# The one-hot rows of the edges' lanes: made by ScalarE in nine operations, or by VectorE in one

## The chip, the cores and the metric

One core of a Trainium2 chip runs the whole program. The metric is the device time of one execution in microseconds (us). Besides TensorE (matmul), VectorE, ScalarE and GpSimd work beside each other, and DMA queues bring data in and out. In profiles they stand as PE (PEld for its weight loads), DVE, ACT, POOL and SP.

## What is computed

The reference is one layer of a graph transformer on 6250 nodes with 512 features and 100,000 edges. Cut to what matters here:

```python
xn = layernorm(x)
h = relu(xn @ W1 + b1) @ W2 + b2
gnn = h + segment_sum(h[dst], src, 6250)          # a sum over each node's edges
x = x + gnn + attention_and_mlp(xn)               # Performer attention, then an MLP with gelu
x = x + haar_ffn(layernorm(x))                    # the tail
```

The edge sum is done on relu(xn @ W1 + b1), which has 256 columns, and W2 is applied afterwards. The rows of the table are gathered for 128 edges at a time, and a matmul with a one-hot matrix adds them to their nodes: row e of that matrix has a 1 in the column of edge e's node within its tile of 125 nodes (its lane), and 0 elsewhere.

## The kernel before

The nodes are handled in 25 steps of 250. **Phase 1** (until about 470 us) makes the k side of the attention and the table of hidden rows, while VectorE sorts the edges by their node. A short **turn** follows. **Phase 2** (531 to 1118 us) makes q, v and y, **phase 3** (1141 to 1751 us) the MLP, and a **tail** the Haar part.

The sorted edges form 440 groups of two times 128 edges (PAIRS); four groups are a batch (BP = 4), and there are 110 batches. A group goes like this. GpSimd gathers its rows into a ring of 12 slots (L592). TensorE multiplies them by two one-hot matrices of 128x125 in float16 (`groups`, L833 to L836), into one of two banks by turns. VectorE adds the bank to the accumulator at an offset read from memory (`add_groups`, L1655). TensorE may start group n when the add of group n-2 is done.

The one-hot matrices of a batch are eight, and stand in one of two buffers `hit`. VectorE makes them all in one compare, 128x1000 (`one_hots`, L1637): the lane numbers 0 to 124 (`iota_h`) against the edges' lanes (`lane_of`). It makes batch q+2 right after the add of the last group of batch q. An edge that has no place in the tile has a lane outside of 0 to 124, and so a row of zeros.

From the turn on each step has eight groups, spread over it. In a step u of phase 2 TensorE's order is: V products (L858 to L860; the first waits for the first y rows of the step before), groups 0 and 1 between and behind them, the first half of the next q products (L721 to L723 and L708 to L710), groups 2 and 3, transposes of q' (L876), the second half of the q products with groups 4 and 5, the y products (L888), and groups 6 and 7 among them. VectorE's order is: the chain that scales q', the adds of groups 0 to 4, `low_parts` (L1432), which splits off the low half of x for step u+2, the reads of the q products (L1556, L1548), the add of group 5, the first y rows (L1756), the add of group 6, the second y rows, the add of group 7, and the row statistics (L1680). With eight groups a step, one compare stands behind the add of group 3 and one behind that of group 7.

ScalarE's order in a step is: two exps (L1147), the copy of the transposed q', called qpT, out of its bank (L1239), and the cast of x's high half for step u+2 (`high_parts`, L1157). `low_parts` waits for that cast. All engines work through their instructions in the order in which they are written.

In phase 3 ScalarE makes norm rows (L1226), two pairs of gelus (L1250) and the copies of the transposed rows (L1139). TensorE makes features (L940) and mlp2 (L949), with groups between. From step 23 on the tail's work joins: copies (L1257, L1262, L1266), gelus (L1272, `tail_gelus`), and the scaling of rows (L1280, `scaled_rows`). There the first mlp2 products of a step also wait for the tail's gelus.

Of the kernel before, what the change touches and what calls it, by code (L numbers as in the profile page):

```python
# [88 lines left out]
TURN, SECOND, BETWEEN, THIRD, LAG = pair_counts()  # L89
LAST = STEPS + LAG  # L90
# [26 lines left out]
def build_program(nc, d):  # L117
    ctx = ExitStack()
    with ctx:
# [111 lines left out]
        row_of, lane_of = in_edge(PAIRS, 2, dt=I32), in_edge(PAIRS, 2, dt=F16)  # L231
# [12 lines left out]
        eps_c = const(2)  # L244
# [72 lines left out]
        def rows(t):  # L317
# [29 lines left out]
        (h_rows, tr, h_t, feat, feat_c, r_up, r_ok, kadd, hk_mm, qn, qt, qtc,  # L347
         y_mm, y_read, zadd, z_ok, m_mm, hits, g_mm, g_add, x_high) = (sem(n) for n in (
            "h_rows", "h_transposed", "hT", "features", "features_copied", "r_read", "r_rows", "kp_added",
# [276 lines left out]
        def _(pe):  # L626
# [195 lines left out]
            def groups(count):  # L822

                for n in range(group_at[0], group_at[0] + count):
                    if n % BP == 0:
                        pe.wait_ge(hits, n // BP + 2)
                    pe.wait_ge(gathered[n % RING], 32 * (n // RING + 1))
                    if n >= 2:
                        pe.wait_ge(g_add, n)
                    for h in (0, 1):  # L830
                        bk, one_hot, row = (BE, BH)[n % 2], hit[n // BP % 2][:, n % BP * 2 + h, :], ring_h[:, n % RING * 2 + h]
                        if h == 0:
                            pe.matmul(bk[0:P, 0:RW], one_hot, row[:, LOW_AND_ONE], start=True, stop=False)  # L833
# [281 lines left out]
        def _(act):  # L1115
# [75 lines left out]
            for t in each_step(1):  # L1191
# [10 lines left out]
                act.activation(acc[0:P, t.u * 2:t.u * 2 + 2, 0:HID], rt[0:P], ACT.Relu).then_inc(r_ok, 1)  # L1202
# [8 lines left out]
            act.wait_ge(ev("rows_listed"), 1)  # L1211
            act.copy(w2_halves[0][:, 0:V_AT].bitcast(F32R), raw_q[:, 0:V_AT]).then_inc(ev("q_high"), 1)
# [17 lines left out]
            def phase2(t, last):  # L1230
                exps(t, lambda t: act.wait_ge(qn, t.u + 1))
                if last:
                    roots(0, EARLY, 12, 11, "early_roots")
                    act.wait_ge(ev("early_scales"), 1)
                    act.wait_ge(sq, 4 * STEPS + 1)
                    norm_rows(each_step(0)[0])
                act.wait_ge(qt, t.u + 2)
                act.wait_ge(y_mm, t.u * 2 + 1)
                act.copy(qpT.rearrange("p a b -> p (a b)"), BF[:, 0:500]).then_inc(qtc, 1)  # L1239
                if t.u + 2 < STEPS:  # L1240
                    high_parts(Step(2, t.u + 2), v_mm, t.u + 1)
            for u in (0, 1):
                high_parts(Step(2, u), w_mm, STEPS * 2)
            for t in each_step(2):
                phase2(t, t.u == STEPS - 1)
# [78 lines left out]
        def _(dve):  # L1324
# [15 lines left out]
            dve.memset(eps_c[:, 0:1], EPS1)  # L1340
            dve.memset(mean_w[:, :], 1.0 / D)
# [220 lines left out]
            def rank_part(u):  # L1562
# [19 lines left out]
                elif u == SORTED + 2:  # L1582
# [3 lines left out]
                    seq(dve.tensor_scalar(tile_at, BH[:, 0:PAIRS], -128.0, None, ALU.mult))  # L1586
# [9 lines left out]
                elif u == SORTED + 4:  # L1596
                    dve.wait_ge(ev("pe_lanes"), 1)
                    for h, bk in ((0, BG), (1, BH)):
                        mm = dve.tensor_tensor(lane_of[:, :, h], bk[:, 0:PAIRS], tile_at, ALU.add)
# [33 lines left out]
            def one_hots(q):  # L1633

                if q > 1:
                    dve.wait_ge(g_mm, BP * (q - 1) + 1)
                dve.tensor_tensor(hit[q % 2], iota_h.unsqueeze(1).to_broadcast([128, 2 * BP, P]),  # L1637
                                  lane_of.rearrange("p n h -> p (n h)")[:, q * 2 * BP:(q + 1) * 2 * BP].unsqueeze(2).to_broadcast(
                                      [128, 2 * BP, P]), ALU.is_equal).then_inc(hits, 1)

            added, offs = [0], {}

            def add_groups(count):

                for n in range(added[0], added[0] + count):
# [10 lines left out]
                    if n % BP == BP - 1 and n // BP + 2 < BATCHES:  # L1656
                        one_hots(n // BP + 2)
# [3 lines left out]
            seq(dve.memset(ring_h[:, :, ONE], 1.0))  # L1661
            one_hots(0)
            one_hots(1)
# [281 lines left out]
```

## Time and profile before

| | us |
|---|---|
| median of 3 runs | 1981.35 |
| lowest, highest | 1980.67, 1992.41 |
| the profiled execution | 1982.79 |
| its span, first to last instruction | 1980.9 |
| mean granted TensorE clock, share of full | 0.933 |

### The profile page before, as it was taken

How to read it: one execution, taken by the hardware profiler on the slowest of the kernel's cores; microseconds unless marked ns; L12 is line 12 of the kernel's file. 1: busy time of each engine (PE TensorE's matmuls, PEld its weight loads, DVE VectorE, ACT ScalarE, POOL GpSimd, SP SyncE). 2: the span in 40 equal slices, each digit the busy share in tenths (PEclk: the TensorE clock that was granted, in tenths of full speed). 3: DMA queues.
4: the chain of work that ended last, by engine and by line, in shares of the span. 5: the costliest groups of instructions: out<-in, count | busy, mean ns of one | idle time of the engine just before them, and what ended most of it. 6: DMA issues, size and time to landing. Idle time of an engine off the chain costs nothing.

```text
span 1980.9 us, 23996 instructions
## 1 busy us (share of the span) xinstructions
PE 1703.0 (86%) x8147; PEld 1277.0 (64%) x8147; DVE 1163.6 (59%) x2430; ACT 437.9 (22%) x900; POOL 1058.6 (53%) x1123
## 2 busy tenths in 40 slices
PE   5999998888889998898989688788888888889997
PEld 4777777776667776776767456555656555655554
DVE  5899999874255565565555433333334333567876
ACT  2233544442011111111111112111112111213443
POOL 3032343234566767676666676666676666655000
PEclk8999999898989999999999789898999988989998
DMA  5132222223355555455555654454454544444332
GB/s 172 37 89 83 84 81 84 71 88 99 93 157 167 168 152 153 153 152 152 153 156 156 178 160 136 152 150 147 149 153 152 154 147 156 149 147 152 120 132 87
DMA packets 87418, 263.55 MB, mean 133 GB/s; under 512 B 18765, under 2 KB 20813, under 8 KB 87298
## 3 DMA queue, kind: packets, MB, share of 16 engines
q0 software_dynamic: 43456, 119.44, 21.3%
q1 hardware_dynamic: 43842, 142.59, 21.2%
q8 instruction: 67, 1.10, 0.2%
q14 instruction: 53, 0.43, 0.1%
HBM read 217.15 MB, written 44.80 MB: 132 GB/s over the span
## 4 chain that ended last, share of the span: by engine, by line
PE 65%; DVE 18%; issue 11%; another core or an unknown queue 3%; DMA 1%; POOL 1%; ACT 1%; DVEq 1%; POOLq 0%; ACTq 0%
PE bank L940 9%; PE bank L949 8%; DVE sb_weights L1375 6%; PE bank L888 4%; PE bank L1014 3%; PE bank L834 2%; PE turn_bank L834 2%; PE bank L858 2%; PE bank L859 2%; PE bank L860 2%; PE bank L709 2%; PE bank L710 2%; PE bank L708 2%; DVE sb_step L1556 2%
## 5 line engine op out<-in xcount | busy, mean ns | idle before, releaser
L592 POOL DMA_INDIRECT sb_weights<-hidden_rows,sb_weights x880 | 894.1, 1016 | 435.8 <-issue 232.0
L1655 DVE TENSOR_TENSOR sb_acc<-sb_acc,bank 125x257 f32 x220 | 92.7, 422 | 368.6 <-PE bank L836 134.8
L940 PE MATMUL bank<-sb_weights,sb_step 128*128 128x250 f32 x800 | 213.2, 427 | 73.4 <-issue 73.0
L940 PEld LDWEIGHTS bank<-sb_weights,sb_step 128*128 128x128 f32 x800 | 171.7, 220 | 104.1 <-issue 78.7
L1655 DVE TENSOR_TENSOR sb_acc<-sb_acc,turn_bank 125x257 f32 x220 | 92.7, 421 | 174.2 <-remote 93.8
L949 PE MATMUL bank<-sb_weights,sb_step 128*125 128x512 f32 x400 | 184.9, 606 | 0.7 <-ACT sb_weights L1312 0.7
L1375 DVE TENSOR_TENSOR sb_weights<-sb_weights 128x512 f32<-128x512 f32 x256 | 172.5, 715 | 3.6
L559 POOL TENSOR_SCALAR sb_const<-sb_const 125x2 f32<-125x2 f32 x25 | 8.9, 354 | 273.7 <-ACT sb_step L1131 273.7
L708 PE MATMUL bank<-sb_w_parts,sb_x_high 128*125 128x512 f32 (+1 forms) x400 | 146.4, 366 | 4.0 <-issue 3.9
L710 PE MATMUL bank<-sb_w_parts,sb_x_low 128*125 128x512 f32 (+1 forms) x400 | 141.0, 353 | 6.0 <-issue 5.9
L709 PE MATMUL bank<-sb_w_parts,sb_x_high 128*125 128x512 f32 (+1 forms) x400 | 141.3, 353 | 2.9 <-issue 2.7
L721 PE MATMUL bank<-sb_w_parts,sb_x_high 128*125 128x256 f32 (+1 forms) x300 | 104.9, 350 | 35.4 <-DVE sb_step L1556 32.2
L1147 ACT ACTIVATE sb_step<-sb_step 125x256 f32<-125x256 f32 x100 | 50.8, 508 | 366.1 <-DVE sb_step L1548 328.0
L1637 DVE TENSOR_TENSOR sb_weights<-sb_const,sb_weights 128x1000 f16<-128x1000 f16 x110 | 131.2, 1194 | 0.0
L949 PEld LDWEIGHTS bank<-sb_weights,sb_step 128*125 128x125 f32 x400 | 73.5, 193 | 76.9 <-issue 75.7
L833 PE MATMUL bank<-sb_weights 128*125 128x257 f16 x220 | 63.5, 289 | 67.7 <-DVE sb_acc L1655 44.3
L1239 ACT COPY sb_step<-bank 128x500 f32<-128x500 f32 x25 | 14.4, 576 | 412.1 <-remote 168.3
L1250 ACT ACTIVATE sb_step<-bank,sb_const 128x250 f32<-128x250 f32 x100 | 41.4, 465 | 278.9 <-remote 158.0
L723 PE MATMUL bank<-sb_w_parts,sb_x_low 128*125 128x256 f32 (+1 forms) x300 | 96.9, 323 | 0.3 <-issue 0.3
L888 PE MATMUL bank<-sb_const,sb_step 128*125 128x512 f32 x200 | 96.7, 607 | 0.3 <-issue 0.3
L722 PE MATMUL bank<-sb_w_parts,sb_x_high 128*125 128x256 f32 (+1 forms) x300 | 96.5, 322 | 0.4 <-issue 0.3
L601 POOL TENSOR_TENSOR sb_step<-sb_step,sb_const 125x2 f32<-125x2 f32 x25 | 17.4, 697 | 143.8 <-DVE sb_step L1824 143.8
(307 smaller groups left out, 3640.1 us busy)
## 6 DMA issues: line engine op xcount, KB each, us to landing
sb_step<-x SPq DMA_DIRECT2D x63, 500.0 KB
sb_step<-x_t SPq DMA_DIRECT2D x50, 500.0 KB
sb_weights<-hidden_rows,sb_weights POOLq DMA_INDIRECT x880
y_rows<-sb_step SPq DMA_DIRECT2D x25, 500.0 KB
sb_step<-y_rows SPq DMA_DIRECT2D x25, 500.0 KB
z_rows<-sb_step SPq DMA_DIRECT2D x25, 500.0 KB
sb_weights<-z_rows SPq DMA_DIRECT2D x13, 500.0 KB
out<-sb_weights SPq DMA_DIRECT2D x13, 500.0 KB
```

What stands on the lines that cost most here:

```text
L592: pool.indirect_dma_start(out=ring[:, n % RING * 2 + h, 0:HID], out_offset=None, in_=table, in_offset=bass.IndirectOffsetOnAxis(ap=row_of[ ...
L708: pe.matmul(bk, high, rhs(0, c), start=c == 0, stop=False)
L709: pe.matmul(bk, high, rhs(1, c), start=False, stop=False)
L710: mm = pe.matmul(bk, low, rhs(0, c), start=False, stop=c == KC - 1)
L721: pe.matmul(outs[c], high, first, start=c == 0, stop=False)
L723: mm = pe.matmul(outs[c], low, first, start=False, stop=c == KC - 1)
L888: mm = pe.matmul(banks[m][0:P, :], qpT[:, c, m * P:(m + 1) * P], pmat[:, c, :], start=False, stop=c == KH - 1)
L940: last = pe.matmul(bk[:, (c % 2) * 250:(c % 2) * 250 + 2 * P], mlp1_w[:, k, c * 128:(c + 1) * 128], hT3[:, t.s, k, :], start=k == 0, stop= ...
L949: mm = pe.matmul((BC, BD)[m][0:P, :], gT3[:, k, m * P:(m + 1) * P], mlp2_w[:, k, :], start=k == 0, stop=k == KC - 1)
L1375: sort_op(dve.tensor_tensor(half(target, c, lo), a, b, op))
L1637: dve.tensor_tensor(hit[q % 2], iota_h.unsqueeze(1).to_broadcast([128, 2 * BP, P]), lane_of.rearrange("p n h -> p (n h)")[:, q * 2 * BP:(q ...
L1655: dve.tensor_tensor(dst, dst, (BE, BH)[n % 2][0:P, 0:RW], ALU.add).then_inc(g_add, 1)
```

## The change

The hits of a batch are no longer made by VectorE but by ScalarE. For each of the eight matrices it makes the distance |iota - lane| (Abs, with minus the lane as the bias column), and then over all eight max(0, 1 - distance) (Relu with scale -1 and bias 1), in place. With whole numbers that is 1 where the lane fits and 0 elsewhere. `lane_of` becomes `less_lane`, minus the lane and float32. A batch now raises `hits` twice, and the Relu waits for the first.

The batches get fixed places in ScalarE's order, where VectorE had made each of them behind an add. A batch q still waits until TensorE is done with batch q-2.

```diff
@@ groups (TensorE)
+                    if n == 0:
+                        pe.wait_ge(ones_in, 2)
                     if n % BP == 0:
-                        pe.wait_ge(hits, n // BP + 2)
+                        pe.wait_ge(hits, n // BP * 2 + 3)
@@ ScalarE
             act.wait_ge(ev("rows_listed"), 1)
+            def one_hots(q):
+                if q == 0:
+                    act.wait_ge(k_mm, STEPS * 2 + 1)
+                if q > 1:
+                    act.wait_ge(g_mm, BP * (q - 1) + 1)
+                for i in range(2 * BP):
+                    mm = act.activation(hit[q % 2][:, i, :], iota_h[:, :], ACT.Abs,
+                                        bias=less_lane[:, q * BP + i // 2, i % 2:i % 2 + 1])
+                mm.then_inc(hits, 1)
+                act.wait_ge(hits, q * 2 + 2)
+                act.activation(hit[q % 2], hit[q % 2], ACT.Relu, scale=-1.0, bias=one_c[:, 0:1]).then_inc(hits, 1)
+            one_hots(0)
             act.copy(w2_halves[0][:, 0:V_AT].bitcast(F32R), raw_q[:, 0:V_AT]).then_inc(ev("q_high"), 1)
@@ phase2 (ScalarE)
                 exps(t, lambda t: act.wait_ge(qn, t.u + 1))
+                one_hots(2 * t.u + 3)
...
                 act.copy(qpT.rearrange("p a b -> p (a b)"), BF[:, 0:500]).then_inc(qtc, 1)
+                one_hots(2 * t.u + 4)
                 if t.u + 2 < STEPS:
                     high_parts(Step(2, t.u + 2), v_mm, t.u + 1)
             for u in (0, 1):
                 high_parts(Step(2, u), w_mm, STEPS * 2)
+            one_hots(1)
+            one_hots(2)
@@ phase 3 (ScalarE)
+            one_hots(2 * STEPS + 3)
             act.wait_ge(v_mm, STEPS + 1)
             copy_hT(steps[0], hT3)
+            one_hots(2 * STEPS + 4)
...
                     gelus(steps[a], 0)
+                    one_hots(2 * STEPS + 5 + 2 * a)
                 if 0 <= b < STEPS:
                     copy_llT(steps[b])
                 if a < STEPS:
                     gelus(steps[a], 1)
+                    one_hots(2 * STEPS + 6 + 2 * a)
...
                 if 0 <= b < STEPS:
                     tail_gelus(steps[b])
                 if a >= STEPS and b + 3 < STEPS:
                     copy_degrees(steps[b + 3])
+                if a >= STEPS and next_hits[0] < BATCHES:
+                    one_hots(next_hits[0])
@@ VectorE
-            def one_hots(q):
-                if q > 1:
-                    dve.wait_ge(g_mm, BP * (q - 1) + 1)
-                dve.tensor_tensor(hit[q % 2], iota_h.unsqueeze(1).to_broadcast([128, 2 * BP, P]),
-                                  lane_of..., ALU.is_equal).then_inc(hits, 1)
...
-                    if n % BP == BP - 1 and n // BP + 2 < BATCHES:
-                        one_hots(n // BP + 2)
...
-            seq(dve.memset(ring_h[:, :, ONE], 1.0))
-            one_hots(0)
-            one_hots(1)
+            dve.memset(ring_h[:, :, ONE], 1.0).then_inc(ones_in, 1)
```

Not shown: a constant column of ones, the sign of `tile_at` and of the subtraction that makes `less_lane`, and the semaphore `r_ok`, which nobody waited for and which becomes `ones_in`.

## Rows read from the trace of the kernel before

**Rows 1.** The page: busy us of each engine, share of the span, instructions

```profile
PE 1703.0 (86%) x8147; PEld 1277.0 (64%) x8147; DVE 1163.6 (59%) x2430; ACT 437.9 (22%) x900; POOL 1058.6 (53%) x1123
```

**Rows 2.** Windows: us; busy of PE, PEld, DVE, ACT, POOL; PEclk, DMA share, GB/s

```profile
531.00:1118.00 587.00, 522.87 (x2882) 414.93 (x2883) 333.26 (x843) 63.92 (x100) 400.83 (x398) 0.95 0.52 156
1141.00:1751.00 610.00, 507.91 (x2216) 362.92 (x2216) 245.79 (x392) 107.72 (x206) 406.04 (x399) 0.92 0.49 151
```

**Rows 3.** The compares' line: duration in ns min/median/max, first and last start, forms

```profile
L1637 DVE TENSOR_TENSOR sb_weights<-sb_const,sb_weights x110: 1190/1194/1234, 472.4 to 1824.8; 128x1000 f16<-128x1000 f16 x110
```

**Rows 4.** Timeline of VectorE, end of step 9: start, us, engine, line

```profile
760.61 0.42 DVE L1655 TENSOR_TENSOR sb_acc<-sb_acc,turn_bank 125x257 f32 x1 [0.20 <-issue]
760.95 1.19 DVE L1637 TENSOR_TENSOR sb_weights<-sb_const,sb_weights 128x1000 f16<-128x1000 f16 x1
762.40 0.42 DVE L1655 TENSOR_TENSOR sb_acc<-sb_acc,bank 125x257 f32 x1 [0.25 <-PE bank L836]
762.74 1.19 DVE L1432 TENSOR_TENSOR sb_x_low<-sb_step,sb_x_high 128x1000 fp32r<-128x1000 f32 x1
...
765.98 0.41 DVE L1655 TENSOR_TENSOR sb_acc<-sb_acc,turn_bank 125x257 f32 x1
766.30 0.74 DVE L1756 SCALAR_TENSOR_TENSOR sb_step<-bank,sb_const 125x512 f32<-125x512 f32 x1
```

**Rows 5.** Timeline of ScalarE, the same stretch

```profile
760.13 0.58 ACT L1239 COPY sb_step<-bank 128x500 f32<-128x500 f32 x1 [17.24 <-issue]
760.61 1.03 ACT L1157 CAST sb_x_high<-sb_step 128x1000 fp32r<-128x1000 f32 x1
```

**Rows 6.** Timeline of TensorE, the same stretch

```profile
767.26 0.48 PE L858 MATMUL bank<-sb_w_parts,sb_x_high 128*125 128x512 f32 x1
```

**Rows 7.** TensorE's waits, 531 to 1118 us: total us, times, longest

```profile
PE bank L833 <- DVE sb_acc L1655: 16.1, 6, 3.8
...
PE turn_bank L833 <- DVE sb_acc L1655: 8.5, 4, 3.9
```

**Rows 8.** TensorE's waits, 1141 to 1751 us

```profile
PE bank L833 <- DVE sb_acc L1655: 18.4, 6, 4.5
```

**Rows 9.** ScalarE by line and shape: busy us, mean ns of one, idle before

```profile
L1157 ACT CAST sb_x_high<-sb_step 128x1000 fp32r<-128x1000 f32 x50 | 51.0, 1022 | 17.6 <-DMA sb_step<-x_t 17.5
L1147 ACT ACTIVATE sb_step<-sb_step 125x256 f32<-125x256 f32 x100 | 50.8, 508 | 366.1 <-DVE sb_step L1548 328.0 <-DVE sb_step L1556 24.3 <-issue 13.8
...
L1272 ACT ACTIVATE sb_step<-bank,sb_const 128x125 f32<-128x125 f32 x50 | 15.5, 362 | 34.9 <-PE bank L1032 28.5 <-remote 6.3
...
L1127 ACT ACTIVATE sb_const<-sb_const 125x2 f32<-125x2 f32 x25 | 5.1, 204 | 0.8
```

**Rows 10.** Timelines of ScalarE and TensorE in step 24 of phase 3

```profile
1752.33 0.62 ACT L1272 ACTIVATE sb_step<-bank,sb_const 128x125 f32<-128x125 f32 x2
...
1753.05 3.24 PE L949 MATMUL bank<-sb_weights,sb_step 128*125 128x512 f32 x7
```

**Rows 11.** Timelines: qpT copy and low half, step 0 and step 22

```profile
548.71 0.57 ACT L1239 COPY sb_step<-bank 128x500 f32<-128x500 f32 x1 [26.34 <-remote]
...
550.53 1.19 DVE L1432 TENSOR_TENSOR sb_x_low<-sb_step,sb_x_high 128x1000 fp32r<-128x1000 f32 x1
...
1070.27 0.58 ACT L1239 COPY sb_step<-bank 128x500 f32<-128x500 f32 x1 [18.35 <-remote]
...
1072.99 1.19 DVE L1432 TENSOR_TENSOR sb_x_low<-sb_step,sb_x_high 128x1000 fp32r<-128x1000 f32 x1
```

**Rows 12.** Timeline of ScalarE in a step of phase 3

```profile
1356.67 0.83 ACT L1250 ACTIVATE sb_step<-bank,sb_const 128x250 f32<-128x250 f32 x2 [5.13 <-PE bank L940]
1365.73 0.57 ACT L1139 COPY sb_weights<-bank 128x500 f32<-128x500 f32 x1 [8.23 <-issue]
```

**Rows 13.** Timeline of ScalarE in the tail

```profile
1793.49 0.37 ACT L1266 COPY sb_step<-bank 126x250 f32<-126x250 f32 x1 [1.52 <-PE bank L988]
1795.58 0.78 ACT L1280 ACTIVATE sb_step<-bank,sb_step 125x512 f32<-125x512 f32 x1 [1.72 <-DVE sb_step L1841]
```

More of the change, by code:

```diff
@@ L89 @@
 TURN, SECOND, BETWEEN, THIRD, LAG = pair_counts()
+assert TURN == BETWEEN == 2 * BP and SECOND == [2 * BP] * STEPS and THIRD[0:STEPS] == [2 * BP] * STEPS
 LAST = STEPS + LAG
@@ L230, in build_program @@
         in_edge = carver(EDGE)
-        row_of, lane_of = in_edge(PAIRS, 2, dt=I32), in_edge(PAIRS, 2, dt=F16)
+        row_of, less_lane = in_edge(PAIRS, 2, dt=I32), in_edge(PAIRS, 2)
         const = carver(CONST)
@@ L243, in build_program @@
         neg_half, pos_half, neg_one, var4 = const(2), const(2), const(2), const(2, 2)
-        eps_c = const(2)
+        eps_c, one_c = const(2), const(1)
         n1g, n1b, n2g, n2b = const(KC), const(KC), const(KC), const(KC)
@@ L346, in build_program @@
             "v_products", "kp_scaled"))
-        (h_rows, tr, h_t, feat, feat_c, r_up, r_ok, kadd, hk_mm, qn, qt, qtc,
+        (h_rows, tr, h_t, feat, feat_c, r_up, ones_in, kadd, hk_mm, qn, qt, qtc,
          y_mm, y_read, zadd, z_ok, m_mm, hits, g_mm, g_add, x_high) = (sem(n) for n in (
-            "h_rows", "h_transposed", "hT", "features", "features_copied", "r_read", "r_rows", "kp_added",
+            "h_rows", "h_transposed", "hT", "features", "features_copied", "r_read", "ones_in_ring", "kp_added",
             "hk_products", "q_scaled", "q_transposed", "qT", "y_products", "y_read", "z_sums", "z_rows",
@@ L1201, in _ @@
                 act.wait_ge(r_up, t.u * 2 + 3)
-                act.activation(acc[0:P, t.u * 2:t.u * 2 + 2, 0:HID], rt[0:P], ACT.Relu).then_inc(r_ok, 1)
+                act.activation(acc[0:P, t.u * 2:t.u * 2 + 2, 0:HID], rt[0:P], ACT.Relu)
                 act.wait_ge(r_st[t.b], 16 * (t.u // 2) + 1)
@@ L1211, in _ @@
             act.wait_ge(ev("rows_listed"), 1)
+            next_hits = [0]
+            def one_hots(q):
+                assert q == next_hits[0]
+                next_hits[0] += 1
+                if q == 0:
[9 more added lines that the diff above has]
+            one_hots(0)
             act.copy(w2_halves[0][:, 0:V_AT].bitcast(F32R), raw_q[:, 0:V_AT]).then_inc(ev("q_high"), 1)
@@ L1340, in _ @@
             dve.memset(eps_c[:, 0:1], EPS1)
+            dve.memset(one_c[:, :], 1.0)
             dve.memset(mean_w[:, :], 1.0 / D)
@@ L1585, in rank_part @@
                     seq(dve.tensor_tensor(pair_at, iota_g, BH[:, 0:PAIRS], ALU.subtract))
-                    seq(dve.tensor_scalar(tile_at, BH[:, 0:PAIRS], -128.0, None, ALU.mult))
+                    seq(dve.tensor_scalar(tile_at, BH[:, 0:PAIRS], 128.0, None, ALU.mult))
                     for q in range(4):
@@ L1598, in rank_part @@
                     for h, bk in ((0, BG), (1, BH)):
-                        mm = dve.tensor_tensor(lane_of[:, :, h], bk[:, 0:PAIRS], tile_at, ALU.add)
+                        mm = dve.tensor_tensor(less_lane[:, :, h], tile_at, bk[:, 0:PAIRS], ALU.subtract)
                     seq(mm)
@@ L1631, in _ @@
                     dve.drain().then_inc(ev("v_split"), 1)
-            def one_hots(q):
-                if q > 1:
-                    dve.wait_ge(g_mm, BP * (q - 1) + 1)
-                dve.tensor_tensor(hit[q % 2], iota_h.unsqueeze(1).to_broadcast([128, 2 * BP, P]),
-                                  lane_of.rearrange("p n h -> p (n h)")[:, q * 2 * BP:(q + 1) * 2 * BP].unsqueeze(2).to_broadcast(
-                                      [128, 2 * BP, P]), ALU.is_equal).then_inc(hits, 1)
             added, offs = [0], {}
```

## The prediction

> **What bounds the kernel now.** I read the page's busy shares first: TensorE 86%, VectorE 59%, ScalarE 22% [rows 1]. On these the change looks free, since ScalarE has the most room and VectorE is relieved. But a share is a mean over stages, so the busy time by stretch comes next. In the second phase (531 to 1118 us, 25 steps of about 23.5 us) TensorE is busy 523 of 587 us, VectorE 333 and ScalarE 64; in the third (1141 to 1751) VectorE is busy 246 of 610 [rows 2]. VectorE isn't short of time in either. What it makes late it makes late by its order, so the question is which chain closes a step. The 110 compares take 131.2 us of VectorE, 1.19 us each [rows 3].
>
> The timeline of the end of one step of phase 2 (step 9) shows the chain [rows 4, 5, 6]. ScalarE copies qpT at 760.13 and, right behind, casts the high half of a later step's x at 760.61. VectorE adds group 3 (760.61), compares (760.95), adds group 4 (762.40), makes the low half of x (L1432, 762.74), reads the q products, adds group 5 (765.98) and makes the first y rows (766.30, until 767.04). TensorE begins the next step's V products at 767.26; they wait for those y rows. From L1432 to the end of the y rows it is 4.3 us, in 17 of the 23 steps the same to 0.1: nothing but VectorE's own work lies between. The next V products begin within 0.1 us of that end in 14 of the 23 steps. So what delays L1432 delays the step.
>
> **The change part by part.** (1) VectorE loses 110 x 1.19 = 131.2 us [rows 3]. Two compares fall in each step of phase 2: one between the adds of groups 3 and 4, one behind group 7, ahead of the row statistics [rows 4]. What they can give back is TensorE's wait for group adds: in phase 2 16.1 + 8.5 us in ten waits [rows 7], in phase 3 18.4 in six [rows 8]. A wait can shrink by the compare ahead of it at most: 10 x 1.19 = 11.9 and 6 x 1.19 = 7.1 us. I take both in full, which favours the change.
>
> (2) ScalarE gets eight Abs of 128x125 and one in-place Relu of 128x1000 per batch. No such Abs from SBUF with a bias column is in the trace. A 128x125 activation from PSUM takes 362 ns and one of 125x256 from SBUF 508 ns; two of the 362 ns kind take 0.62 us together, so neighbours overlap by 0.1 [rows 9, 10]. I take 0.40 alone and 0.30 in a row: 7 x 0.30 + 0.40 = 2.5 us. The Relu is nearest to the 1000-wide cast, 1.02 us; with its bias column 1.1 [rows 9]. With 0.05 for its wait on the eight, a batch is 3.65 us, 110 of them 402 us: ScalarE goes from 438 to some 840 us. Bounds: below, eight at the 204 ns of a two-wide operation and 1.0, so 2.6; above, eight at 508 ns without overlap and 1.1, so 5.2.
> The Trainium skill (ScalarE: Activation LUTs, What ACT_TABLE_LOAD costs) gives 280 ns + 0.833 ns a column for an activation with a bias column and 93 ns of overlap in a row; by that, as an estimate, a batch is 3.5 us and the sum some 3 us smaller. The same page (Rules for kernel authors) says to give relu and add to VectorE, not ScalarE; the row of the compare, 1.19 us against my 3.65, goes that way.
>
> (3) The place of the batches in ScalarE's queue. In phase 2 batch 2u+3 stands behind the exps: ScalarE is idle for 17 us ahead of the qpT copy [rows 5], so it costs nothing. Batch 2u+4 stands between the qpT copy and the cast of x's high half. Its hits are not needed until the next step's first groups; the cast behind it is needed at once, by L1432, and behind L1432 on VectorE wait the q reads, group 5's add and the y rows. New start of L1432 after the copy's start: 0.48 (copy) + 3.65 + 1.03 (cast) + 0.04 = 5.2 us. Before it is, for steps 0 to 22: 1.8, 1.8, 5.1, 5.6, 5.2, 2.6, 1.5, 3.7, 2.6, 2.6, 1.8, 1.8, 3.3, 4.1, 3.5, 2.9, 6.1, 2.0, 1.8, 1.8, 1.8, 1.8, 2.7 us (first and last of 23 in [rows 11]). The shortfalls to 5.2 sum to 52.9 us. Where the V products began later than the y rows' end, that slack is taken off: 47.6 us remain. The compare that goes ahead of group 4 doesn't help here, because L1432 then waits for the cast.
>
> (4) Phase 3. Batch 55+2a stands between the two pairs of gelus: the second begins after 5.1 us of idleness, so 3.65 us fit. Batch 56+2a has from 1357.5 to the hT copy at 1365.73 [rows 12]. Nothing is lost, but for steps 23 and 24, where the tail's gelus follow the second batch: they were made at 1752.33 to 1752.95, and mlp2 starts on them at 1753.05 [rows 10]. The batch waits for group 1 of the step (whose matmuls run up to that point, some 1753.2), then 3.65 + 0.62 us: mlp2 at 1757.5, 4.4 us late, twice 8.8 us. In the five tail steps with a batch, it stands ahead of the row scaling, which began at 1795.58, 1.7 us after the copy ahead of it ended [rows 13]: 3.65 - 1.7 = 1.9 late, of which about 1.2 is made good by the compare VectorE no longer makes. I take 0.6 each, 3 us.
>
> (5) At the turn batch 0 delays the q cast by 3.65 us; VectorE comes to its use only behind four group adds that wait for gathers. Nothing there, and the small edits (less_lane's sign, the constant column, the waits in TensorE's queue) cost nothing for the same reason: they are single operations ahead of long waits.
>
> Sum: 47.6 - 11.9 - 7.1 + 8.8 + 3 = +40 us. The profiled span is 1980.9 us, its own time 1982.8, the median of the three runs 1981.35; the stretches outside the steps are left alone, so I add to the median: **2022 us**.
>
> **The rivals.** *Hidden (0.23).* TensorE has 64 us without a record in phase 2, and its results often reach the other engines some us behind their records, as if work were queued in it. Then a later y row eats part of that and not the step. If half of the 47.6 passes: 24 - 19 + 12 = +17; if a quarter, 12 - 19 + 12 = +5. Between them lies 1992 us. Against it: the V products start on the y rows' end in most steps.
> *VectorE's relief wins (0.10).* The cast isn't what ends L1432's wait, because TensorE's results come later than it anyway (as in steps 2, 3, 4 and 16, where the old distance is 5 us or more), and all of TensorE's waits for adds go: -24.6 - 18.4 + 12 = -31, so 1950 us. It decides if the distance of copy to L1432 stays under 3 us or the batch takes under about 1.3 us. The row of the cast alone, 1.02 us for as many elements as the Relu, speaks against the latter.
> *The clock falls too (0.12).* PEclk in phase 2 is 0.95 [rows 2], so the granted clock goes to its lower level (1.2 GHz) now and then. If each longer wait brings one more such stretch, say 1.5 us lost in each of 23 steps, it is +40 + 35 = 2057 us. The upper price of a batch, 5.2 us, gives about the same: the shortfalls are then 80.7, the sum +76.
>
> **How the numbers follow.** Forecast 0.55, hidden 0.23, relief 0.10, clock or dear batch 0.12. The low price of a batch (2.6 us) gives 27.5 - 19 + 6 + 1.5 = +16, 1997 us. The forecast's own range is 1997 to 2045. With the rivals the range is 1980 to 2050: it leaves out the relief and the upper half of the last case. Faster by over 1% (under 1961.5): 0.09. Within 1%, which is about what a measurement of this kernel can tell from no change: 0.23. Slower by over 1% (over 2001.2): 0.68.
>
> **What would show it.** ScalarE busy near 840 us with nine operations a batch, VectorE near 1032. The 110 batches last 3.5 to 3.8 us from first Abs to the end of the Relu. In phase 2 the distance of the qpT copy to L1432 is 5.2 us or more in all steps, VectorE's idle time ahead of L1432 ends on the cast, and the steps go from 23.5 to about 25 us. TensorE's wait for the adds of groups 0 and 1 shrinks. Step length of phase 3 stays within 0.5 us but for steps 23 and 24, where mlp2 waits 4 us. Wrong would be: no new wait ahead of L1432, a batch under 2.6 us, or activation table loads at each batch, which no row leads me to expect.

## The result, and the profile after

The changed kernel takes 2010.42 us (median of four runs, 2001.43 to 2014.85), the kernel before 1983.59 beside it: a ratio of 1.0106, 95% interval 1.0076 to 1.0136. Slower by 1%. The profiled execution has a span of 2013.0 us against 1980.9, so 32.1 us are to be placed; it is the slowest of the four, and the medians are 26.8 us apart. Of the runs further down, one of late_on_dve (1892.06 us) and one of the kernel before beside it (1885.42 us), both at a granted clock of 0.84 where the others have 0.95 or more, are left out of medians and ratios.

The page of the changed kernel, busy us of each engine (before: [rows 1]), and its windows over phases 2 and 3 (before, and the columns: [rows 2]):

```profile
PE 1717.1 (85%) x8147; PEld 1279.4 (64%) x8147; DVE 1043.5 (52%) x2321; ACT 819.8 (41%) x1890; POOL 1028.0 (51%) x1123
...
531.00:1118.00 587.00, 515.21 (x2840) 406.08 (x2838) 271.69 (x769) 227.34 (x528) 377.22 (x387) 0.94 0.51 150
1141.00:1751.00 610.00, 498.00 (x2153) 353.47 (x2152) 184.22 (x330) 282.00 (x654) 390.29 (x399) 0.90 0.50 153
```

VectorE gave up 120 us, ScalarE took on 382, and TensorE, which nobody touched, has less done in the same stretch: 2840 matmuls instead of 2882 in the first, 2153 instead of 2216 in the second. ScalarE's two new lines, by shape (busy us, mean ns of one | idle before, ended by):

```profile
L1226 ACT ACTIVATE sb_weights<-sb_const,sb_weights 128x125 f16<-128x125 f16 x880 | 266.6, 389 | 58.5 <-remote 23.2 <-PE turn_bank L839 19.6 <-PE bank L839 8.5
L1230 ACT ACTIVATE sb_weights<-sb_weights,sb_const 128x1000 f16<-128x1000 f16 x110 | 124.1, 1128 | 3.6
```

The end of one step of phase 2 (step 9), ScalarE, VectorE and TensorE, to be laid beside [rows 4, 5, 6]:

```profile
778.62 0.58 ACT L1260 COPY sb_step<-bank 128x500 f32<-128x500 f32 x1 [11.96 <-remote]
779.09 2.42 ACT L1226 ACTIVATE sb_weights<-sb_const,sb_weights 128x125 f16<-128x125 f16 x8
781.55 1.13 ACT L1230 ACTIVATE sb_weights<-sb_weights,sb_const 128x1000 f16<-128x1000 f16 x1
782.59 1.01 ACT L1160 CAST sb_x_high<-sb_step 128x1000 fp32r<-128x1000 f32 x1
```

```profile
783.63 1.20 DVE L1463 TENSOR_TENSOR sb_x_low<-sb_step,sb_x_high 128x1000 fp32r<-128x1000 f32 x1 [2.91 <-ACT sb_x_high L1160]
...
787.21 0.74 DVE L1775 SCALAR_TENSOR_TENSOR sb_step<-bank,sb_const 125x512 f32<-125x512 f32 x1
```

```profile
788.01 0.78 PE L861 MATMUL bank<-sb_w_parts,sb_x_high 128*125 128x512 f32 x1
```

The predicted chain is there: copy 778.62, batch to 782.68, cast, low half at 783.63 (5.0 us behind the copy), the y rows until 787.95, the next V products at 788.01. In 19 of 23 steps the distance from copy to low half is 5.0 us. The steps, however, hardly grew.

I cut the span at five places that every trace has: the first V products of phase 2, those of its step 24, the first gelu of phase 3, the first gelus of steps 23 and 24. In us, from the timelines (the pairs further down belong to the experiments):

| stretch | before | after | | second chip: before_again | after_again | | half_before | half_after |
|---|---|---|---|---|---|---|---|---|
| start to phase 2 | 531.4 | 539.3 | +8.0 | 520.2 | 520.0 | | 522.8 | 536.1 |
| phase 2, 24 steps | 568.3 | 579.3 | +11.0 | 491.3 | 505.3 | | 476.2 | 503.8 |
| to the first gelu | 47.1 | 55.2 | +8.1 | 48.7 | 35.2 | | 30.6 | 30.4 |
| phase 3, 23 steps | 571.8 | 562.9 | -9.0 | 493.7 | 480.4 | | 439.2 | 439.1 |
| its step 23 | 24.9 | 32.5 | +7.6 | 28.1 | 33.9 | | 26.3 | 33.4 |
| to the end | 237.4 | 243.8 | +6.4 | 235.4 | 240.9 | | 231.1 | 240.6 |
| span | 1980.9 | 2013.0 | +32.1 | 1817.5 | 1815.8 | | 1726.1 | 1783.3 |

And within a step of phase 2, the mean distances, us:

| | before | after | before_again | after_again | half_before | half_after |
|---|---|---|---|---|---|---|
| V products to qpT copy | 15.63 | 14.37 | 11.60 | 11.39 | 11.41 | 11.42 |
| copy to low half | 2.96 | 5.21 | 4.25 | 5.15 | 3.77 | 5.09 |
| low half to next V products | 5.03 | 4.66 | 4.66 | 4.58 | 4.67 | 4.55 |

So in the first pair the late cast cost 23 x 2.25 = 51.8 us, and 24 x 1.26 = 30 us came back ahead of the copy and 9 behind it. The compares are gone from VectorE; was it that? The experiments say no for another kind of chip, and for this kind with half of the gathers; with all of them it stays open.

One oddity of the first pair matters below. The copy waits for the last transpose (L876). In these two traces it starts 2.4 us (before) and 2.1 us (after) on the mean behind the recorded end of that transpose, and up to 8.1 us; in each of the other twelve traces it is 0.04 us in every step. So TensorE's records run ahead there of what the other engines see, and 0.3 of the 1.26 us is a change of this lag.

### The profile page after: what moved, and what is told of

It reads as the page before. It is cut to its first block, busy times and chain, and to the rows that moved or that the text cites. A ratio compares the mean times of both kernels' runs of the same rounds, so it can differ in the third digit from the quotient of the medians.

```text
span 2013.0 us, 24878 instructions
## 1 busy us (share of the span) xinstructions
PE 1717.1 (85%) x8147; PEld 1279.4 (64%) x8147; DVE 1043.5 (52%) x2321; ACT 819.8 (41%) x1890; POOL 1028.0 (51%) x1123
## 4 chain that ended last, share of the span: by engine, by line
PE 59%; DVE 16%; issue 12%; ACT 5%; another core or an unknown queue 4%; POOL 1%; DMA 1%; DVEq 0%; POOLq 0%; ACTq 0%
PE bank L943 10%; PE bank L952 8%; DVE sb_weights L1406 6%; PE bank L861 2%; ACT sb_weights L1226 2%; PE bank L891 2%; DVE sb_step L1587 2%; PE bank L862 2%; PE bank L863 2%; PE bank L1017 2%; PE turn_bank L837 2%; PE bank L837 2%; PE bank L709 2%; PE bank L710 2%
## 5 line engine op out<-in xcount | busy, mean ns | idle before, releaser
L593 POOL DMA_INDIRECT sb_weights<-hidden_rows,sb_weights x880 | 862.3, 980 | 497.2 <-issue 224.5
L1226 ACT ACTIVATE sb_weights<-sb_const,sb_weights 128x125 f16<-128x125 f16 x880 | 266.6, 389 | 58.5 <-remote 23.2
L952 PE MATMUL bank<-sb_weights,sb_step 128*125 128x512 f32 x400 | 192.8, 627 | 14.7 <-issue 8.5
L709 PE MATMUL bank<-sb_w_parts,sb_x_high 128*125 128x512 f32 (+1 forms) x400 | 141.0, 353 | 0.9 <-issue 0.6
L710 PE MATMUL bank<-sb_w_parts,sb_x_high 128*125 128x512 f32 (+1 forms) x400 | 136.6, 341 | 1.9 <-issue 1.9
L711 PE MATMUL bank<-sb_w_parts,sb_x_low 128*125 128x512 f32 (+1 forms) x400 | 135.9, 340 | 0.4 <-issue 0.4
L722 PE MATMUL bank<-sb_w_parts,sb_x_high 128*125 128x256 f32 (+1 forms) x300 | 105.8, 353 | 35.2 <-DVE sb_step L1587 32.6
L836 PE MATMUL turn_bank<-sb_weights 128*125 128x257 f16 x220 | 62.5, 284 | 80.2 <-issue 41.3
L1230 ACT ACTIVATE sb_weights<-sb_weights,sb_const 128x1000 f16<-128x1000 f16 x110 | 124.1, 1128 | 3.6
L836 PEld LDWEIGHTS turn_bank<-sb_weights 128*125 128x125 f16 x220 | 30.6, 139 | 109.5 <-issue 107.8
```

What stands on the lines that cost most here:

```text
L593: pool.indirect_dma_start(out=ring[:, n % RING * 2 + h, 0:HID], out_offset=None, in_=table, in_offset=bass.IndirectOffsetOnAxis(ap=row_of[ ...
L709: pe.matmul(bk, high, rhs(0, c), start=c == 0, stop=False)
L710: pe.matmul(bk, high, rhs(1, c), start=False, stop=False)
L711: mm = pe.matmul(bk, low, rhs(0, c), start=False, stop=c == KC - 1)
L722: pe.matmul(outs[c], high, first, start=c == 0, stop=False)
L952: mm = pe.matmul((BC, BD)[m][0:P, :], gT3[:, k, m * P:(m + 1) * P], mlp2_w[:, k, :], start=k == 0, stop=k == KC - 1)
```

## The experiments

**A swap that puts the cast first, and three kernels beside it.** The swap:

```
                 act.copy(qpT..., BF[:, 0:500]).then_inc(qtc, 1)
-                one_hots(2 * t.u + 4)
                 if t.u + 2 < STEPS:
                     high_parts(Step(2, t.u + 2), v_mm, t.u + 1)
+                one_hots(2 * t.u + 4)
```

> The changed kernel with one pair of statements swapped: in phase 2 ScalarE casts sb_x_high for step u+2 straight behind the qpT copy, and makes the batch 2u+4 behind the cast instead of ahead of it. Theory A (the late cast sets the end of each step of phase 2; VectorE's relief is real): copy to low parts falls from 5.2 us to 1.6-2.2 us, 23 steps, while the copy keeps coming at 14.4 us behind the V products; phase 2 shortens by 40-75 us against the changed kernel, total 1940-1970 us, faster than the kernel before (1983). Theory B (the late cast is covered: the adds or the batches on ScalarE set the step, and the copy comes later when the cast comes earlier): copy to low parts falls, the V products to copy time grows by as much, total within 10 us of 2010.

The delay alone, in the kernel before (four more casts, one waiting for the other):

```
                 act.copy(qpT..., BF[:, 0:500]).then_inc(qtc, 1)
                 if t.u + 2 < STEPS:
+                    (the two waits of high_parts)
+                    for i in range(4):
+                        act.copy(xh[...], xt[...]).then_inc(idle, 1)
+                        act.wait_ge(idle, 4 * t.u + i + 2)
                     high_parts(Step(2, t.u + 2), v_mm, t.u + 1)
```

> The kernel before (VectorE compares) with ScalarE delayed alone: in phase 2 the cast of sb_x_high is issued five times in a row instead of once, so that its last end comes about 4.2 us later; nothing else moves, the result is the same. Theory A: copy to low parts goes from 2.96 us to about 5.8 us, and each of the 23 steps grows by nearly that, 45-65 us in all, total 2030-2048 us. Theory B (the cast has cover): under 20 us, total below 2003 us.

VectorE's relief alone:

```
-                    if n % BP == BP - 1 and n // BP + 2 < BATCHES:
-                        one_hots(n // BP + 2)
```

(and TensorE waits for the first two batches only)

> The kernel before with VectorE's compares left out from the third batch on (108 of 110; the later groups multiply by the first two batches' one-hots, so the sums of the edges are others): VectorE's relief alone, with ScalarE as it was. Theory A (the relief is worth what the changed kernel's phase 2 shows: 1.26 us a step ahead of the copy, 0.38 us behind it, and the low parts start earlier where the compare had delayed them): V products to copy 14.4 us, copy to low parts 1.6-2.2 us, phase 2 shorter by 40-70 us, phase 3 by 2-10 us, total 1910-1945 us. Theory B (the prediction's sizes: 11.9 us in phase 2 and 7.1 us in phase 3): total 1955-1970 us.

Both engines:

```
+ON_DVE = 2 * STEPS + 3
...
                     dve.tensor_tensor(dst, dst, ..., ALU.add).then_inc(g_add, 1)
+                    if n % BP == BP - 1 and ON_DVE <= n // BP + 2 < BATCHES:
+                        compared(n // BP + 2)
```

(compared(q) is the old compare; ScalarE's batches from number 53 on are gone, the cast is first)

> The changed kernel with the cast first as in cast_first, and with the batches from number 53 on (those made behind phase 2) compared by VectorE behind each fourth group as in the kernel before. Theory A (beyond phase 2 ScalarE's batches cost 6.4 us in the tail and some us at the change of phases, and give back little in phase 3): 5-15 us under cast_first, V24 to the first gelu back from 55 to 47-50 us. Theory B (those differences are not the batches': they come and go from run to run): within 3 us of cast_first.

Measured: cast_first 1813.08 us, late_cast 1894.14, no_compare 1797.11, both_engines 1808.19, and the kernel before beside them 1821.45. No absolute expectation can be read any more: this was another chip, on which the kernel before is 8% faster. As ratios to the kernel before: cast_first 0.9962 (0.9948 to 0.9976), late_cast 1.0388 (1.0364 to 1.0413), no_compare 0.9869 (0.9853 to 0.9886), both_engines 0.9927 (0.9911 to 0.9944).

late_cast stands by theory A in direction. Its four extra casts take 4.24 us, but the cast had to wait for its load anyway, so the distance from copy to low half grows by 3.19 us, from 4.25 (before_again, below) to 7.44. In all it costs 73 us: phase 2 is 95.8 us longer (587.1 against 491.3), and the way to the first gelu 14.8 us shorter. TensorE waits there for the late adds and nothing else (waits, 560 to 1090 us):

```profile
PE turn_bank L833 <- DVE sb_acc L1660: 75.5, 22, 8.6
```

A cast that is late by 3 to 4 us does set the step. Part of the price is the clock: phase 2 of late_cast has 95.6 us at the lower level (1.2 GHz) and that of before_again 13.7; PEclk over the phase is 0.92 and 0.99. So the longer waits of TensorE came with more of the lower clock here, as the prediction's rival had it.

The relief alone is worth 24 us; theory A, with 40 to 70 for phase 2 alone, is out. Theory B, the prediction's own sizes (11.9 and 7.1 us), comes near: phase 2 is 9.8 us shorter than in before_again (481.5 against 491.3) and the first 23 steps of phase 3 are 9.1 us shorter (484.6 against 493.7). V products to copy is 11.37 us without compares and 11.60 with them: 0.2 us a step, not 1.26. So on this chip there is next to no relief ahead of the copy. both_engines is 5 us under cast_first, as theory A said; its last stretch is 235.1 us against 240.8 and its step 23 of phase 3 26.4 against 34.3, but its first 23 steps there are 10.5 us longer (495.3 against 484.8).

**The changed kernel itself on such a chip.** Four more kernels, to have both traces there. late_on_dve is both_engines with the swap undone.

> The changed kernel once more, unaltered, beside the others of this call. Two things are open. First, the last four kernels ran beside a kernel before of 1821 us, not 1983: there TensorE ran phase 2 without the gaps of 0.7 us that the first traces show. If the late cast costs there what the delayed cast cost (71 us for 4.24 us a step, 97.5 us of delay over 23 steps, so 0.73 us for each us), the changed kernel's 3.6 us a step cost 60 us against cast_first: about 1865-1875 us beside 1821, slower by 2-3%. If only its ratio of 1.011 carries over: about 1841 us. Second, the turn (+8.0 us) and the change from phase 2 to 3 (+8.1 us) were longer in the first trace: if the batches made there cost it, both return (first V product at least 6 us after that of the kernel before, and V24 to the first gelu at least 6 us longer); if it is variation from run to run, they don't.

> The kernel before once more, unaltered, for a trace on the same chip as the other kernels: the same time as its repeats beside them. For the turn and the change of phases: if its first V product (531.4 us in the first trace) and V24 to the first gelu (47.1 us) lie within 2 us of the changed kernel's of this call, the 16 us found there in the first pair of traces are not the change's.

> The changed kernel with the batches from number 53 on compared by VectorE as in the kernel before, and phase 2 as changed (batch 2u+4 ahead of the cast). Against the changed kernel of this call: if ScalarE's batches cost 6.4 us in the tail and 8 us at the change of phases and give back 1.4 us in phase 3, 13 us less; if both_engines (5 us under cast_first, 1808 against 1813) tells the size, 3-7 us less.

> The changed kernel with the cast ahead of batch 2u+4, once more, so that the swap is measured beside the changed kernel itself. If the late cast is what makes the changed kernel slow: at least 30 us under the changed kernel of this call and 0.4% under the kernel before, as in the first call. If the chip matters (TensorE's gaps of 0.7 us return), V products to copy comes back to 14 us, and the swap gains less in ratio, 15-40 us.

Measured beside 1823.50 us for the kernel before: after_again 1818.52 (ratio 0.9979, 0.9967 to 0.9992), late_on_dve 1817.20 (0.9958, 0.9939 to 0.9977), cast_first_again 1813.12 (0.9941, 0.9920 to 0.9962), before_again 1819.32 in its one run. Both of my times for after_again were wrong: on this chip the change costs nothing. Nor did the 16 us of the first pair return: the turn is equal, and the way to the first gelu turned its sign. The expectation that the cast-first swap gains 30 us failed with it, it gains 5. late_on_dve was to save 3 to 13 us. What it saves can't be told from nothing: 1.3 us by the medians, 4 by the ratios, whose intervals overlap. Its step 23 and last stretch are 5.8 and 5.9 us shorter than in after_again, and its first 23 steps of phase 3 13.6 us longer (494.0). The table of stretches shows how the zero comes about: phase 2 is 14.0 us longer and the way to the first gelu 13.5 us shorter.

That the compares cost something in phase 3 shows in eight traces of this kind of chip. The first 23 steps take 491.8 to 495.3 us in the four kernels whose VectorE compares there (before_again, late_cast, both_engines, late_on_dve) and 480.4 to 484.8 us in the four others. GpSimd's gathers start 1.30 to 1.31 us apart on the mean in the former and 1.28 to 1.29 in the latter. TensorE waits for gathered rows there, so this is a likely way for the compares to act; no run tests it.

Two rows explain the small loss in phase 2. ScalarE at the same place in before_again, then in after_again:

```profile
764.00 0.58 ACT L1239 COPY sb_step<-bank 128x500 f32<-128x500 f32 x1 [11.78 <-PE bank L876]
766.93 1.03 ACT L1157 CAST sb_x_high<-sb_step 128x1000 fp32r<-128x1000 f32 x1 [2.36 <-DMA sb_step<-x_t]
```

```profile
769.62 0.58 ACT L1260 COPY sb_step<-bank 128x500 f32<-128x500 f32 x1 [7.57 <-PE bank L879]
770.10 2.43 ACT L1226 ACTIVATE sb_weights<-sb_const,sb_weights 128x125 f16<-128x125 f16 x8
772.56 1.13 ACT L1230 ACTIVATE sb_weights<-sb_weights,sb_const 128x1000 f16<-128x1000 f16 x1
773.59 1.01 ACT L1160 CAST sb_x_high<-sb_step 128x1000 fp32r<-128x1000 f32 x1
```

Here TensorE reaches the copy 11.3 us behind the V products in most steps, and the load of the transposed x, which can't be issued before those products have read the buffer (6.3 us behind their start), lands at 14.3 us. The cast waits for it: in before_again it starts 0.02 to 0.03 us behind the landing in each of the steps 1 to 22. The batch of 3.6 us fills a hole of 2.4 us. Only the rest delays the low half, 0.9 us a step on the mean, instead of 2.25.

Two more rows explain where it goes back, TensorE's waits for gathered rows from 985 to 1500 us, in before_again and in after_again:

```profile
PE turn_bank L833 <- DMA sb_weights<-hidden_rows,sb_weights: 39.0, 25, 3.9
```

```profile
PE turn_bank L836 <- DMA sb_weights<-hidden_rows,sb_weights: 14.3, 9, 2.6
```

GpSimd issues the gathers. Its line from 560 to 1500 us, in the first trace and in before_again:

```profile
L592 POOL DMA_INDIRECT sb_weights<-hidden_rows,sb_weights x630 | 637.3, 1012 | 304.5 <-issue 165.7 <-remote 71.3 <-PE bank L836 42.6
```

```profile
L592 POOL DMA_INDIRECT sb_weights<-hidden_rows,sb_weights x716 | 719.5, 1005 | 222.1 <-issue 196.4 <-PE bank L836 16.7 <-PE turn_bank L836 8.9
```

716 gathers in 940 us are 1.31 us each, and a step has 16: 21.0 us. Phase 2 of before_again runs at 20.5 us a step, that of after_again at 21.05. The kernel before runs ahead of its gathers and pays behind phase 2; the changed kernel runs at their pace and pays less, and later. The packets of the gathers' queue show it: in before_again the rows of a group have landed some 20 us ahead of their use early in phase 2, and 2 us at its end and through phase 3; in after_again it is still 21 us at the end of phase 2, and 1 to 3 us only from the middle of phase 3 on. A hidden 14 us.

**Half of the gathers, and a slower TensorE.** The last four. half_ leaves out the second gather of each pair but for the first lap of the ring (12 pairs; the expectation's 13th lap is a slip), and TensorE waits for one landing less in each later lap; slow_ repeats one product of TensorE twice in each step:

```
-                    for h in (0, 1):
+                    for h in (0, 1) if n < RING else (0,):
                         pool.indirect_dma_start(
```

```
+                for _ in range(2 if m == 0 and t.u > 0 else 0):
+                    gram_product((BA, BG)[m], t, m, w2_grams)
                 gram_product((BA, BG)[m], t, m, w2_grams).then_inc(k_mm, 1)
```

> The kernel before with TensorE slowed in phase 2: ahead of the copy, in each of 24 steps, the product of the next step's queries (12 matmuls, 1.85 us) is issued three times instead of once. Alone it is the base for slow_after. With 3.7 us more, V products to copy goes from 11.3 to 15.0 us, the load of the transposed x (14.3 us behind the V products in the trace of the second chip) lands ahead of the copy, copy to low parts falls from 4.25 to 2.6-2.9 us, a step from 19.8 to about 22.4, phase 2 longer by 60 us, total 1865-1885 us where the kernel before takes 1821.

> The changed kernel with TensorE slowed in the same way. Theory A (the change's late cast is free only where the cast waits for its load anyway; with TensorE's part of a step longer, the load is there before the copy): copy to low parts 5.0 us against 2.6-2.9, steps 24.6 against 22.4, and nothing of it is given back, as POOL needs only 20.9 us for a step's gathers: 35-55 us over slow_before, slower by 2-3%. Theory B (VectorE's relief, 1.3 us a step ahead of the copy in the first pair of traces, comes back with the slower TensorE): 10-25 us over slow_before. Theory C (the change is free on this chip in any case): within 5 us.

> The kernel before with half of the gathers left out (the second of each pair's two, from the 13th lap or so of the ring on its old rows stay: the edges' sums are others, all matmuls remain). POOL's issuing, 1.31 us a gather and 20.9 us a step, no longer sets a pace, and there is less DMA traffic. Alone it is the base for half_after; the waits of TensorE for gathered rows, 30 us in phase 3, are gone: total 1775-1800 us.

> The changed kernel with the same half of the gathers left out. Theory A (the changed kernel's phase 2 is 14 us longer, its tail 5.5 us longer, and POOL's pace hides that, since the kernel before waits for gathered rows instead): with the pace gone the change costs at least 12 us over half_before, and up to 55 us if the load of the transposed x lands earlier with less traffic (copy to low parts 5.0 against 2.6 us). Theory B (the two kernels are equal for another reason, the relief of VectorE): within 5 us of half_before.

By chance these ran on a chip like the first one, as far as the time goes: the kernel before takes 1991.37 us there. (The lag of the copy in the first pair is in none of these four traces.) Measured: slow_before 1999.66 (1.0053), slow_after 2011.99 (1.0104), half_before 1727.71 (0.8689), half_after 1784.21 (0.8963).

half_before, expected at 1775 to 1800 us, is the largest surprise of the study. Half of the gathers gone are worth 264 us here, and phase 2 then takes 476.2 us, near the 491.3 of before_again on the second chip. The windows from 560 to 1000 us (columns as in [rows 2]) of half_before, slow_before and before_again:

```profile
560.00:1000.00 440.00, 437.48 (x2595) 354.15 (x2594) 298.17 (x757) 58.24 (x89) 179.05 (x178) 0.99 0.43 132
```

```profile
560.00:1000.00 440.00, 426.81 (x2546) 349.96 (x2545) 242.34 (x616) 45.64 (x72) 294.56 (x290) 0.98 0.52 154
```

```profile
560.00:1000.00 440.00, 430.60 (x2510) 344.48 (x2509) 290.74 (x740) 54.99 (x84) 335.46 (x331) 0.98 0.58 177
```

The difference between the two kinds of chip is visible in TensorE's own timeline. In the first trace of before, inside one run of products that wait for nothing (step 9 of phase 2), and in half_before:

```profile
756.25 0.27 PE L876 MATMUL bank<-sb_const,sb_step 125*128 125x125 f32 x1 [0.26 <-issue]
756.95 0.42 PE L876 MATMUL bank<-sb_const,sb_step 125*128 125x125 f32 x2 [0.44 <-issue]
757.66 0.39 PE L721 MATMUL turn_bank<-sb_w_parts,sb_x_high 128*125 128x512 f32 x1 [0.29 <-issue]
759.06 0.40 PE L722 MATMUL turn_bank<-sb_w_parts,sb_x_high 128*125 128x512 f32 x1 [1.01 <-issue]
```

```profile
739.84 0.36 PE L708 MATMUL bank<-sb_w_parts,sb_x_high 128*125 128x256 f32 x1
740.04 0.28 PE L709 MATMUL bank<-sb_w_parts,sb_x_high 128*125 128x256 f32 x1
740.16 0.28 PE L710 MATMUL bank<-sb_w_parts,sb_x_low 128*125 128x256 f32 x1
740.28 0.28 PE L708 MATMUL bank<-sb_w_parts,sb_x_high 128*125 128x256 f32 x1
```

Starts 0.12 to 0.23 us apart are normal; the stalled ones are 0.70 and 1.40 apart, with no semaphore in between. Counting matmuls inside products that start over 0.62 us behind their neighbour at the higher clock, phase 2 has 18 such places in before and 24 in slow_before, 9 in after, and none in half_before, half_after, before_again, after_again or any other trace of the second kind of chip. slow_after has none either. Most of its steps take 24.15 us, the length of the chain (14.75 + 5.01 + 4.4 us).

The four kernels of this kind of chip that make all gathers have nearly the same step: phase 2 takes 23.7 us a step in before, 24.1 in after, 24.3 in slow_before, with 3.7 us more of matmuls in each (60 us in all were expected, 16 came), and 24.4 in slow_after. What a kernel adds is mostly absorbed. It looks like a pace, but not one of rows that come too late. By the packets of the gathers' queue, the rows of every group of phase 2 landed some 20 us or more before TensorE began it in all four, and nearly so in phase 3; and GpSimd itself waits longer for TensorE to free slots of the ring (560 to 1500 us, the first trace, then before_again):

```profile
POOL sb_weights L592 <- PE bank L836: 42.6, 25, 4.1
POOL sb_weights L592 <- PE turn_bank L836: 25.0, 24, 2.1
```

```profile
POOL sb_weights L592 <- PE bank L836: 16.7, 46, 3.0
POOL sb_weights L592 <- PE turn_bank L836: 8.9, 27, 1.0
```

What sets that step is open. So is what makes the stalls fewer in after and slow_after: it can be the late cast or the missing compares, and neither late_cast nor no_compare ran on this kind of chip.

With half of the gathers the change costs what its chain says: 19.8 against 21.0 us a step, and 56.5 us in all: 27.6 in phase 2, 13.3 in the turn, 16.6 in step 23 and the tail. Theory A of half_after holds (at least 12 us), though not by the load: the cast starts 2.7 us behind the copy in half_before and 3.1 in before_again, so copy to low half is 3.77 us, not 2.6; and no theory had the 13.3 of the turn. Of slow_after's theories, B gave the number (12.3 us, expected 10 to 25). Its reason, VectorE's relief on the chain, doesn't hold in general: V products to copy is shorter (14.85 against 16.00 us) in the pair with stalls and the same (11.42 and 11.41) in the pair without them, though VectorE lost its compares in both. TensorE's waits from 560 to 1000 us in slow_before and in slow_after:

```profile
PE bank L722 <- issue: 4.0, 10, 1.0
PE bank L723 <- issue: 3.7, 7, 1.1
```

```profile
PE turn_bank L838 <- DVE sb_acc L1680: 17.8, 18, 2.1
```

Stalls without a cause in the one, waits for the late adds in the other, and the same step.

## Why the prediction was right

The time (2022 foretold, 2010.42 measured, in the range) and the direction are right. Point by point, the first pair of traces unless another is named:

- *A batch, 3.65 us.* Right: 2.42 for the eight Abs, 1.13 for the Relu, 3.50 to the cast's start (779.09 to 782.59). ScalarE went from 438 to 820 us (840 foretold), VectorE to 1043.5 (1032). The Abs takes 389 ns (0.40 foretold), the Relu 1.128 (1.1). By the Trainium skill (ScalarE: Activation LUTs, What ACT_TABLE_LOAD costs) the estimates would be 384 and 1113 ns; the trace agrees to 2%.
- *Late low half, 52.9 us of shortfalls.* Right: 51.8 us, 5.0 to 6.2 us in every step where 5.2 or more was foretold. No other term was read so closely off single steps.
- *Less slack and relief: 35.7 us for phase 2.* Wrong in size: 11.0. I let the shortfalls pass nearly in full, since V products start on the end of the y rows. They did, and still the steps grew little, because the distance from V products to copy shrank by 1.26 us: it was not a sum of work but held stalls that gave way. TensorE's waits for the adds did not shrink as foretold but went from 24.6 [rows 7] to 34.5 us, and yet the copy came earlier:

```profile
PE turn_bank L836 <- DVE sb_acc L1678: 32.8, 14, 3.7
...
PE bank L836 <- DVE sb_acc L1678: 1.7, 1, 1.7
```

  The step of the prediction that failed is the one that took only the compares, at 11.9 us, for what could give; 40.8 us of the 51.8 came back. The rival *hidden* said that, "as if work were queued", at half; the true share was less still.
- *Steps 23 and 24 of phase 3, +8.8 us, and the tail, +3.* The 8.8 is nearly exact. TensorE's idle time at mlp2, 1700 to 1800 us, is twice 4.2:

```profile
PE bank L952 <- issue: 8.5, 2, 4.2
```

  Step 23 and the rest to the end hold both delays and the tail, 11.8 us foretold; measured 14.0, and 11.3 and 16.6 in the other two pairs of the table. With ScalarE's late batches back on VectorE (late_on_dve) they are 28.1 and 235.0 us, as in before_again.
- *Phase 3's relief, -7.1 us.* The size is near: -9.0 in the first 23 steps, -10.3 in the slow_ pair, and on the second kind of chip 7 us or more between the two groups of traces above. It needs all of the gathers: in the half_ pair those steps take 439.2 and 439.1 us. On the second kind TensorE waited for rows, not only for adds as foretold; how the compares act on the first is open. "Nothing is lost" was wrong for two copies of ScalarE that a batch now precedes. From 1141 to 1751 us TensorE's features wait for the hT copies:

```profile
PE bank L943 <- ACT sb_weights L1142: 20.2, 6, 7.6
```

  And for the fc1 copy of step 2 TensorE waited 0.7 us before (L1312), and from 1200 to 1260 us of the changed kernel's trace:

```profile
PE bank L952 <- ACT sb_weights L1342: 6.2, 1, 6.2
```

- *Turn, 0 us.* Wrong on this kind of chip: +8.0, and +3.8 and +13.3 in the slow_ and half_ pairs; -0.1 on the other kind. TensorE's kptv products in after, in the turn, and in after_again:

```profile
505.75 1.01 PE L904 MATMUL bank<-sb_step,sb_w_parts 128*128 128x256 f32 x2 [0.82 <-issue]
507.87 2.02 PE L904 MATMUL bank<-sb_step,sb_w_parts 128*128 128x256 f32 x3 [1.11 <-issue]
512.10 1.29 PE L904 MATMUL bank<-sb_step,sb_w_parts 128*128 128x256 f32 x2 [2.21 <-issue]
```

```profile
498.69 3.72 PE L904 MATMUL bank<-sb_step,sb_w_parts 128*128 128x256 f32 x16
```

  Sixteen products in 3.7 us, or stalls of up to 2.8 us between two of them. The stalls are in the traces of before too, but later (508 to 519 us, in other products). Why the changed kernel meets them earlier and longer is open; no run here moved a batch in the turn alone.
- *To the first gelu.* No term; +8.1 and +11.2 (slow_ pair, 43.3 and 54.5), -0.3 with half of the gathers, -13.5 on the second chip. On the second chip it is where the kernel before pays for running ahead of its gathers. What in it is due to batches 53 and 54, which no run moved by themselves on the first kind of chip, is open.
- *Clock.* PEclk went from 0.95 to 0.94 in phase 2 and from 0.92 to 0.90 in phase 3. Phase 2 has 64.8 us at the lower level in 17 stretches where it had 54.6 in 15, not one more in each step: as an estimate at most 5 us, half of the difference, where the rival had 35. The whole trace has 302.5 us at the lower level where it had 266.8, which can be worth up to 18 us by the same estimate; how much of the 32 it is, no run shows. On the second kind of chip late_cast did what the rival said.

So the 32 us are 14 in step 23 and behind it (shown: in all pairs, and on the second kind of chip gone with the late batches back on VectorE), 11 in phase 2 (what is left of a 52 us delay: its full price of 27.6 us shows with half of the gathers, and what takes the rest up with all of them, stalls, the lag of the copy or a pace, isn't shown), 16 around the turn and the change of phases, less 9 in phase 3. That the right total came from a phase 2 three times too dear and two places priced at nothing is luck.

The best version measured that makes all sums right is the one with the cast first and VectorE comparing from batch 53 on: 0.9927 (0.9911 to 0.9944) on the second kind of chip. On the first kind it wasn't run.

## What to carry to other kernels

An operation put ahead of a critical one costs only what isn't covered by the latest other thing that this one waits for: look for the load's landing, not only for the engine before. Ask next what pace something off the chain (here 16 gathers a step) allows, and how far ahead of their use its results land: where that is 20 us all the way, it sets nothing, and where it falls to 2 us, the steps can't be shorter. And put long work for an idle engine behind what others wait for, not ahead of it: the swap of two statements took phase 2's loss away and more (505.3 to 482.5 us, 491.3 in before_again) even where only 5 us of it reached the end.

## What the hardware showed that I had not expected

- The same program took 1981 to 1991 us on some chips and 1821 to 1824 on others, and the sign of a 1% change went with it: 1.0106 on the one, 0.9979 on the other.
- On the slower ones TensorE stalls between matmuls of one product, often by 0.70 or 1.40 us from start to start, waiting for nothing that the profile shows. Half of the gathers left out removed all such places in phase 2 on the same kind of chip, and 264 us of 1991. What joins gathers to TensorE there was not found. It isn't that rows come late, since they land some 20 us ahead. The list of waits alone can't say so: in the four of them that have all gathers, over half of the gathers' landing events are missing, and a wait for one would stand under another name.
- An indirect DMA occupies GpSimd for 1.0 us. On both kinds of chip most of them start 1.25 us behind the one before (the median); the means are 1.31 us on the faster chips and 1.49 on the slower (940 us / 630), where GpSimd waits for free slots of the ring. By the median, as an estimate, the 880 take at least 1100 us.
